# Expert stage of a mixture-of-experts kernel: weights and rows sent by SyncE in turn, pad rows laid in the last batch

## What is computed

```
x = layernorm(x + attention(x))
top_idx = argmax(x @ gate_w.T + gate_b + expert_bias)
for e in range(8):
    y = relu(x @ w1[e] + b1[e]) @ w2[e] + b2[e]      # 128 -> 512 -> 128
    out = out + (top_idx == e) * y
x = layernorm(x + out)
```

## Time and profile before

| | |
|---|---|
| median of 3 runs | 440.21 us (438.69 to 440.54) |
| profiled execution | 439.83 us, of it span 438.1 us |
| TensorE busy | 416.3 us (95%) |
| VectorE busy | 362.1 us (83%) |
| ScalarE busy | 356.4 us (81%) |
| POOL busy | 152.1 us (35%) |

### The profile page before, as it was taken

How to read it: one execution, slowest core, us unless ns; L and a number is a source line. 1 busy time by engine, 2 the same in 40 slices (tenths; PEclk the granted TensorE clock), 3 DMA queues, 4 the chain that set the end, 5 groups by cost and what they waited for, 6 DMA issues and landing times. The chain is left out here.

```text
span 438.1 us, 12324 instructions
## 1 busy us (share of the span) xinstructions
PE 416.3 (95%) x4235; PEld 230.2 (53%) x4235; DVE 362.1 (83%) x824; ACT 356.4 (81%) x568; POOL 152.1 (35%) x164
## 2 busy tenths in 40 slices
PE   8899999999999999999999999998999899699993
PEld 6533344444443444444444444443444698599992
DVE  3978897999998889999987999999878578377764
ACT  3979999999998999998899999998889564376661
POOL 8221001315213013512401314212001466688887
PEclk9889999999999999999999999999899999899998
DMA  5268510668671135544500760674410255477640
GB/s 154 50 167 195 162 49 1 144 145 227 145 170 30 45 87 126 123 112 103 133 2 6 164 149 27 142 170 133 125 39 2 73 140 156 146 223 197 200 136 20
DMA packets 33005, 50.62 MB, mean 116 GB/s; under 512 B 5627, under 2 KB 16545, under 8 KB 32944
## 3 DMA queue, kind: packets, MB, share of 16 engines
q1 hardware_dynamic: 25488, 36.51, 34.1%
q10 hardware_dynamic: 5184, 9.05, 7.3%
q0 software_dynamic: 2272, 4.27, 2.9%
HBM read 21.35 MB, written 5.33 MB: 61 GB/s over the span
## 5 line engine op out<-in xcount | busy, mean ns | idle before, releaser
L1032 ACT ACTIVATE prob<-ring 128x1024 f32<-128x1024 f32 x288 | 274.5, 1039 | 25.8 <-PE ring L1224 25.0
L1242 PE MATMUL o_acc<-prob,v_stat 128*32 128x512 f32 (+3 forms) x1536 | 155.8, 501 | 2.9 <-DVE prob L705 2.1
L1224 PE MATMUL ring<-queries,keys 32*128 32x512 f32 (+3 forms) x1536 | 126.8, 385 | 0.4 <-DVE queries L665 0.4
L1224 PEld LDWEIGHTS ring<-queries,keys 32*128 32x128 f32 x1536 | 71.0, 187 | 71.4 <-issue 48.0
L691 DVE TENSOR_SCALAR prob<-prob 128x2048 f32<-128x2048 f32 x64 | 77.4, 1220 | 7.2 <-ACT prob L1032 6.8
L705 DVE SCALAR_TENSOR_TENSOR prob<-prob,mask_hi 128x1024 f32<-128x1024 f32 (+1 forms) x80 | 82.2, 1028 | 0.0
L1120 ACT ACTIVATE prob<-ring,b1T 128x128 f32<-128x128 f32 x156 | 44.6, 368 | 35.6 <-issue 16.4
L704 DVE TENSOR_SCALAR prob<-prob 128x1024 f32<-128x1024 f32 (+1 forms) x80 | 64.7, 808 | 6.6 <-ACT prob L1032 6.1
L584 POOL DMA_INDIRECT by_expert<-xrow,index x32 | 40.1, 1254 | 78.1 <-DVE index L800 71.0
L1242 PEld LDWEIGHTS o_acc<-prob,v_stat 128*32 128x32 f32 x1536 | 34.1, 109 | 57.2 <-issue 39.5
L565 POOL TENSOR_TENSOR rstd<-var_eps,const 128x4 f32<-128x4 f32 x8 | 16.4, 2048 | 92.0 <-DVE var_eps L748 92.0
(11 more groups left out here) (117 smaller groups left out, 343.5 us busy)
## 6 DMA issues: line engine op xcount, KB each, us to landing
queries<-query_parts SPq DMA_DIRECT2D x60, 256.0 KB, 4.0
v_stat<-in_w ACTq DMA_DIRECT2D x34, 256.0 KB
keys<-key_parts SPq DMA_DIRECT2D x60, 128.0 KB, 2.5
queries<-by_expert SPq DMA_DIRECT2D x39, 66.0 KB
xrow<-in_x_rows SPq DMA_DIRECT2D x8, 264.0 KB, 4.4
xT<-in_x_T SPq DMA_DIRECT2D x8, 256.0 KB, 3.0
v_stat<-in_w SPq DMA_DIRECT2D x5, 256.0 KB
out<-prob,queries POOLq DMA_INDIRECT x39
```

The costliest lines, as they stand in the source:

```text
L1032: act.activation(prob[u % P_SLOTS][:, 2 * half:2 * half + 2, :].rearrange("p h s -> p (h s)"), slot(("score", u, half))[:], ACT.Exp, scale ...
L1224: last = pe.matmul(out[:, j % 2 * QC + off:j % 2 * QC + off + w], keys[hg][r, kt * P:(kt + 1) * P], queries[hg][r, qc, part, QC - w:QC], s ...
L1242: last = pe.matmul(o_acc[j * VW:(j + 1) * VW, QC - w:QC], v_stat[b % 2][:, hg, kt, j, :], prob[u % P_SLOTS][:, j, off:off + w], start=begi ...
```

## The change

SyncE sends everything in the expert stage: after five weights it sends twelve row tiles (`RING`), and then in iteration `c` the weights of tile `c + 5` and, from tile 12 on, the rows of tile `c + 4` (`ROWS_AHEAD`). ScalarE sends nothing and reads the expert of each tile itself. The pad rows are laid in batch 3, once batches 0 to 2 are scattered: for each expert 1024 + 128 rows behind its last row, straight from a DRAM input, and the last batch's tokens are later scattered over them, for which POOL waits for `padded`. `pad_at` is taken at the start of `early_plan`. The last half is scattered after tiles 8 and 9.

```diff
-ROUTE_AT = {9: (0, 1), 10: (2, 3)}
-PAD_AT = 9
-PADS_ACT = 2
+ROUTE_AT = {8: (0, 1), 9: (2, 3)}
+PAD_ROWS = S + P
+ROWS_AHEAD = 4
...
                 if b == B - 1:
                     sp.wait_ge(queries_out, len(PROJECTS))
                     sp.dma_start(b2[:], io["b2"].to_broadcast([P, E * D])).then_inc(mlp_in, 16)
+                    for q in range(Q):
+                        sp.wait_ge(routed[q], b * QT * 16)
+                    sp.wait_ge(pad_ready, 1)
+                    for e in range(E):
+                        at = sp.value_load(pad_at[0:1, e:e + 1], min_val=0, max_val=DUMMY - PAD_ROWS)
+                        sp.dma_start(by_expert[bass.ds(at, PAD_ROWS), :], io["pad_rows"]).then_inc(padded, 16)
...
+            def load_up(c):
+                e = sp.value_load(expert_tab[0:1, c:c + 1], min_val=0, max_val=E - 1)
+                if c >= W1_SLOTS:
+                    sp.wait_ge(up_mm, c - W1_SLOTS + 1)
+                sp.dma_start(w1_tile[c % W1_SLOTS], io["w1"].rearrange("e d f -> (e d) f")[bass.ds(e * D, D), :]
+                             ).then_inc(w1_in[c % W1_SLOTS], 16)
+
             for c in range(W1_AHEAD):
-                e = sp.value_load(expert_tab[0:1, c:c + 1], min_val=0, max_val=E - 1)
-                sp.dma_start(w1_tile[c], io["w1"].rearrange("e d f -> (e d) f")[bass.ds(e * D, D), :]
-                             ).then_inc(w1_in[c], 16)
-            for c in range(EARLY_TILES):
+                load_up(c)
+            for c in range(RING):
                 load_tile(c)
-            pad(sp, range(E - PADS_ACT))
-            for q in range(Q):
-                sp.wait_ge(routed[q], B * QT * 16)
-            sp.wait_ge(padded, E * 16)
-            sp.wait_ge(planned, 4)
-            for c in range(EARLY_TILES, TILES):
-                load_tile(c)
+            for c in range(TILES):
+                if c + W1_AHEAD == EARLY_TILES:
+                    sp.wait_ge(planned, 4)
+                if c + W1_AHEAD < TILES:
+                    load_up(c + W1_AHEAD)
+                if c + ROWS_AHEAD == EARLY_TILES:
+                    for q in range(Q):
+                        sp.wait_ge(routed[q], B * QT * 16)
+                if RING <= c + ROWS_AHEAD < TILES:
+                    load_tile(c + ROWS_AHEAD)
...
                 pool.wait_ge(index_ready, g + 1)
+                if g // Q == B - 1:
+                    pool.wait_ge(padded, E * 16)
...
                 dve.wait_ge(carried, (B - 1) * Q + 1)
+                dve.tensor_copy(pad_at[:], next_row[:]).then_inc(pad_ready, 1)
...
-                if c + W1_AHEAD == EARLY_TILES:
+                if c + 1 == EARLY_TILES:
                     act.wait_ge(planned, 4)
-                if c + W1_AHEAD < TILES:
-                    load_up(c + W1_AHEAD)
                 for kind, i in tail_job(c):
                     job(kind, i)
-                if PAD_AT <= c < PAD_AT + PADS_ACT:
-                    pad(act, [E - PADS_ACT + c - PAD_AT])
```

More of the change, by code:

```diff
@@ L265, in build @@
         next_row = sb("next_row", [P, E])
-        pad_row = sb("pad_row", [P, ROW])
         pad_at = sb("pad_at", [P, E], I32)
@@ L319, in build @@
         kq_in = [[sem(f"kq_in{i}{c}") for c in range(NQC)] for i in range(NHG)]
-        out_w_in, gate_in, mlp_in, pad_in = sem("out_w_in"), sem("gate_in"), sem("mlp_in"), sem("pad_in")
+        out_w_in, gate_in, mlp_in = sem("out_w_in"), sem("gate_in"), sem("mlp_in")
         ident_ready, mask_ready, upper_ready = sem("ident_ready"), sem("mask_ready"), sem("upper_ready")
@@ L387, in last_unit @@
             return k // NQC * NU + LAST_OF_QC[k % NQC]
[L389 to L396, removed]
         def is_direct(b, hg, c):
@@ L492, in _ @@
             load_rows(0, 1)
-            sp.dma_start(pad_row[:], io["pad_rows"]).then_inc(pad_in, 16)
             for b in range(B):
@@ L510, in _ @@
                 if b == 0:
-                    sp.wait_ge(pad_in, 16)
-                    sp.dma_start(by_expert[DUMMY:DUMMY + P, :], pad_row[:]).then_inc(dummy_out, 16)
+                    sp.dma_start(by_expert[DUMMY:DUMMY + P, :], io["pad_rows"][0:P, :]).then_inc(dummy_out, 16)
                     sp.dma_start(w2[:].rearrange("p (e c) d -> p e c d", e=E),
@@ L921, in late_plan @@
                     dve.wait_ge(carried, B * Q + 1)
-                    dve.tensor_copy(pad_at[:], next_row[:]).then_inc(pad_ready, 1)
                     dve.tensor_tensor(tokens_of[:], next_row[:], const[:, CONST["region"]], ALU.subtract).then_inc(plan, 1)
@@ L1098, in xT_evac @@
                 act.activation(xsT[c % 2][:], bank[c % 2][:, 0:P], ACT.Copy).then_inc(xsT_ready, 1)
[L1100 to L1110, removed]
             def relu(c):
-                e = experts.pop(c) if c in experts else act.value_load(expert_tab[0:1, c:c + 1], min_val=0, max_val=E - 1)
+                e = act.value_load(expert_tab[0:1, c:c + 1], min_val=0, max_val=E - 1)
                 act.wait_ge(up_mm, c + 1)
@@ L1472 @@
         "x_rows": with_ids(x.reshape(N, D), np.arange(N)).reshape(2 * B, S // 2, ROW),
-        "pad_rows": with_ids(np.zeros((P, D), np.float32), N + np.arange(P)),
+        "pad_rows": with_ids(np.zeros((PAD_ROWS, D), np.float32), N + np.arange(PAD_ROWS)),
         "w_latent": latent_weights(a), "w_kq": key_query_weights(a),
```

## The result

The changed kernel took 445.9 us (median of four runs, 445.44 to 447.87), the kernel before 440.4 in the same series (438.69 to 441.81): a ratio of 1.015 with a 95% interval of 1.011 to 1.019. It is slower by some 6 us, near the 444.9 us forecast.

A forecast was written before the change was run, and what follows sets the result against it. TensorE bounds the steady expert stage at 1.91 us per tile, after a hole; SyncE would become the bound. Tile 38 +5.7, tail -0.65, sum +5.05 on 439.83 gives 444.9 us, range 436.0 to 452.5.

The forecast's parts named there:

- Step 1: Expert stage: eight pad transfers leave, closing their part of the 366 to 384 us hole; tile 16's rows 3.2 us early.
- Step 2: Last batch, from about 302 us: 4.87 MB of pad copies stay hidden before the first `turn_x`; cost zero.
- the upper of my rates: Pad copies, DRAM to DRAM: bound from the trace's fastest microsecond, 418 GB/s, 11.7 us; the other was 196 GB/s.
- Step 3: Expert stage: ScalarE no longer sends 34 weight loads, some 0.34 us each; worth nothing in the steady part.
- Step 4: Expert stage: SyncE sends both at 1.22 us per transfer, 2.44 us per tile against TensorE's 1.91, and becomes the bound.
- Step 5: POOL: last rows scattered after tiles 8 and 9, not 9 and 10, ending near 375.2 us; effect zero.
- Step 6: POOL's wait for pads is already passed; SyncE's wait for all scatters ahead of tile 17 costs zero, at most 1.
- The sum: Tile 17's weights at 374.9, 44 steps of 1.22 us, 1.8 landing: tile 38's `turn_x` at 430.5, +5.7; total +5.05.
- The tail: After tile 38's `turn_x`: the same 13.3 us of work, less 0.65 because POOL is no longer behind.
- TensorE busy for 80%: Sign in the new profile: TensorE busy some 80% of 380 to 425 us, idling ahead of `turn_x`.
- the first `turn_x` must not move: Sign at the expert stage's start, 340.55 us: if it moves, the forecast is wrong.
- SyncE keeps up: Expert stage: a transfer costs SyncE 0.95 us or less, TensorE stays the bound, 436.0 us; chance 0.15.

The follow-up runs named there:

- experiment 1: Both kernels run again unedited, giving each a second trace: changed kernel 1.0115 of the kernel before, which took 438.2 us.
- Experiments 6: Kernel before with SyncE sending the weights too, in the changed kernel's order; pads and last scatters stay late: ratio 1.018 to the kernel before.
- 4b: Changed kernel with each tile's row address read twice by SyncE, no transfer more: ratio 1.036 to the kernel before.
- 4a: Changed kernel with each weight tile sent by SyncE as two halves, same bytes: ratio 1.032 to the kernel before.
- experiment 2: Changed kernel with ScalarE sending the weights of tiles 5 to 38 again, pads and scatters as changed: ratio 0.996 to the kernel before, in both series.
- 5a: Changed kernel with ScalarE sending the weights again and the last scatters back at tiles 9 and 10: ratio 0.999 to the kernel before.

## Right and wrong, step by step

The mechanism and the size were right: SyncE, sending both, became the bound. That the sum came so near is in part luck, since several of its terms were off in opposite directions.

- *Step 1, the pads leave (worth about 3 us in the forecast): wrong.* I read the pads' 10.73 us and the hole off one trace, where they stood side by side, and took one for the cause of the other. Most of what those pads took beyond the 6.8 us of the second trace was SyncE's drawn-out instructions (experiment 1). Such instructions stand in the changed kernel's first trace as well, where no pads are left in this stage, so they need no pads. In the second trace of the kernel before the rows of tile 17 waited for the last scatter, landed 2.5 us after the pads. The pads' move alone measured 0.999. `turn_x` of tile 16 was not near 378 but at 382.21 in the first trace; in the second it stood 37.3 us after the first `turn_x`, where the forecast had 37.5, but in the second trace of the kernel before that was 36.4 already.
- *Step 2, eight copies of 608 KB hidden: right.* Their bytes went at this pace (stretches of the changed kernel, last column GB/s):
```profile
302.00:306.00 4.00, 2.88 (x36) 1.01 (x38) 4.00 (x5) 3.29 (x5) 0.00 (x0) 1.00 1.27 377
306.00:310.00 4.00, 4.00 (x60) 2.09 (x60) 4.00 (x7) 3.96 (x5) 0.00 (x0) 1.00 0.93 342
```
  nearer to the upper of my rates. Experiments 6 (pads late) and 4b (pads early) have the same clock from stretch to stretch, so their starts can be compared; for each the stretch from 302 to 336 us and the first `turn_x`:
```profile
302.00:336.00 34.00, 32.54 (x369) 14.62 (x373) 29.17 (x54) 29.80 (x34) 2.15 (x1) 1.00 0.27 74
```
```profile
336.85 0.44 PE L1337 MATMUL ring<-ident,queries 128*128 128x128 f32 x2
```
```profile
302.00:336.00 34.00, 32.39 (x365) 14.50 (x365) 29.16 (x54) 29.64 (x34) 2.15 (x1) 1.00 0.63 209
```
```profile
337.00 0.44 PE L1332 MATMUL ring<-ident,queries 128*128 128x128 f32 x2
```
  Nearly three times the bytes, 0.15 us.
- *Step 3, ScalarE free of sending is worth nothing: held.* With all weights on ScalarE TensorE is the bound at 1.90 us.
- *Step 4, the price of a transfer: right, slightly too high.* 1.174 us measured over 44 steps against 1.22, so 2.0 us too many; without hitches 1.13 to 1.14. The sentence of the Trainium skill (DMA: Bandwidth & Descriptors, "Issuing engines are not separate DMA queues") quoted in the prediction, by which sending is usually small relative to the DMA itself, does not hold here: sending took 1.1 us, where the rows landed 1.7 to 3.8 us after they were sent (median 1.9, kernel before in experiment 1), and two sends did not fit in a tile's 1.9 us. Experiments 4a and 4b show the sequencer's time alone at work. The 600 ns that the Trainium skill gives as the floor of `tensor_load` (same page, "Latency and other measured facts") isn't what was seen here either, 0.27 us a read in the profile and 0.6 us for a read with its range check in experiment 4b.
- *Step 5, the scatters one tile earlier, zero: most likely wrong.* They release the rows of tile 17 in the kernel with weights on ScalarE; experiment 2 against 5a puts them at about 1 us, with overlapping intervals. It is a gain that the changed kernel can't show, as SyncE sets its end.
- *Step 6, SyncE's wait for the scatters, zero to 1: too low.* 1.5 us in the second trace. For one thing a scatter's landing was mis-sized: I took 1.8 us after the instruction's end, and in the first trace of experiment 2 the last one ended at 376.3 us and had landed at 378.9. For another SyncE was early at tile 17's weights, 32.5 us after the first `turn_x`, where my sum had 34.4. In the first trace, at 38.1 us, the hole had made it late and the wait was nothing.
- *The sum.* First `turn_x` to last: forecast 430.5 - 340.55 = 89.95, measured 92.7 and 89.1. In the first trace SyncE's start with the weights of tile 17 was 0.9 us later than forecast (375.76 against 374.9), which is 3.7 us of delay behind the first `turn_x`, in which the hole stands, less the 2.9 by which the whole stage began earlier (337.68 against 340.55), neither of which was forecast; the pace 2.0 us less, the last rows needed 2.95 us to their `turn_x` instead of 1.9: 430.37 against 430.5. The tail was 13.6 us, against 13.3 before and 12.65 in the forecast: it kept the 0.65 us that I took off. The last tiles came at 1.90 us again, since SyncE has no weights to send at the end, and POOL was behind as before, last variance and inverse deviation:
```profile
438.33 0.15 DVE L997 TENSOR_SCALAR y_var<-y_mean 128x1 f32<-128x1 f32 x1
439.14 0.57 POOL L612 TENSOR_TENSOR y_rstd<-y_var,const 128x1 f32<-128x1 f32 x1
```
- *The signs.* TensorE busy for 80% was wrong: it was 94%, and the count of matmuls fell by 16%. That the first `turn_x` must not move was a bad sign to name: it moves by as much between two executions of one kernel (last section).
- *The rival "SyncE keeps up"* named 436.0 us, on a base of 440.2. Experiment 2, in which what it supposes is made true by other means, gives 0.996 x 440.2 = 438.5: less than half the gain, since I had the pads' part too high.

## What to carry to other kernels

A queue that sends transfers with computed addresses has a price per transfer, read off a burst in which it waits for nothing; set it against the time of one step of the loop before giving that queue a second transfer per step. Below the threshold the other engine keeps the pace, though half the weights on SyncE still read 1.3 and 2.8 us above none, within overlapping intervals. Above it each further instruction on that queue, even one that sends nothing, shows at the end, here with some 70 to 90% of its price. A hole and a burst of transfers that stand side by side in one trace need not be cause and effect: look for the wait that ended last, and take a second trace of the same kernel before pricing the hole.

## What the runs showed of the hardware

- The same program starts its last stage up to 5 us apart from one execution to the next. The granted clock between 20 and 30 us was 0.70 in one execution of the kernel before and 1.00 in the other, the first `turn_x` at 340.55 and 338.61; in one of experiment 2 it was 0.79, with 0.90 from 302 to 336 us, and 342.05. The two executions of the kernel before:
```profile
20.00:30.00 10.00, 10.00 (x88) 4.46 (x84) 7.22 (x9) 7.26 (x9) 2.65 (x2) 0.70 0.79 194
```
```profile
20.00:30.00 10.00, 9.69 (x108) 4.24 (x108) 8.80 (x11) 9.15 (x11) 2.60 (x2) 1.00 0.85 204
```
  Ahead of 30 us the two kernels differ in one load of pad rows only. Differences of stage starts are therefore no evidence for an edit unless the clock rows agree. Where they do, starts agree too: the four executions with 0.70 to 0.73 in that stretch started the stage at 340.29 to 340.58, and the four with 1.00 there and 0.95 from 302 to 336 us at 338.61 to 339.06, across seven different kernels.
- In two executions TensorE stood still for 5.5 and 5.6 us while the last scatters were under way, and ScalarE for longer. In the changed kernel's first trace (366 to 384 us) ScalarE's wait was put down to no engine of the trace:
```profile
ACT prob L1117 <- remote: 6.7, 1, 6.7
```
  and the trace of experiment 5a has the same, 7.0 us. In the other traces TensorE's holes there were shorter, or a named wait for rows. In the first traces of both kernels some of SyncE's register instructions took 0.7 us each shortly before or in the hole. What it is stays open: that it stood beside the scatters is an observation, not a test.
- One transfer of 66 KB with a computed address needs about 1.1 us of SyncE although the DMA instruction takes 0.34: the rest is the read of the table (0.27), the address, the check and the waits.
